# Routed expert tiles: rows gathered by a table of each slot's row number and share, results added by accumulating scatter

## The reference, cut to what matters

```python
x = x + attention0(layernorm(x), ctx)        # 32 heads of 16
x = x + ffn0(layernorm(x))                   # the part that the change touches
x = x + attention1(layernorm(x), ctx)        # 32 heads of 128
x = x + ffn1(layernorm(x))                   # low-rank adapters

def ffn0(x):                                 # x: 1024 tokens x 512
    scores = sigmoid(x @ gate_w.T) + bias    # 16 experts
    topk_w, topk_idx = top_k(scores, 4)
    topk_w = topk_w / sum(topk_w)            # the share of each chosen expert
    cw = one_hot(topk_idx) weighted by topk_w
    z = silu(x @ Wg[e].T) * (x @ Wu[e].T)    # for each expert e, width 256
    out = sum over e of (z * cw[:, e]) @ Wd[e].T
    return out + (silu(x @ Sg.T) * (x @ Su.T)) @ Sd.T     # the shared expert
```

## Time and profile before

| | us |
|---|---|
| median of 3 runs | 1466.79 (1466.39 to 1470.21) |
| profiled execution, its own time | 1462.81 |
| its span, first to last instruction | 1461.2 |
| PE busy | 1275.9 (87%) |
| DVE busy | 965.8 (66%) |
| ACT busy | 812.3 (56%) |
| POOL busy | 389.6 (27%) |
| mean granted TensorE clock | 0.949 of full |
| DMA | 181.72 MB, mean 124 GB/s |

### The profile page before, as it was taken

The page is one execution under the profiler, slowest core; times in us unless marked ns, Lnnn a source line. Parts: engine busy times, 40 slices in busy tenths (PEclk is TensorE's granted clock), DMA queues, the critical chain, the costliest instruction groups (busy, mean ns, idle before and its releaser), DMA issues.

```text
span 1461.2 us, 18404 instructions
## 1 busy us (share of the span) xinstructions
PE 1275.9 (87%) x6250; PEld 1019.9 (70%) x6250; DVE 965.8 (66%) x1889; ACT 812.3 (56%) x2152; POOL 389.6 (27%) x685
## 2 busy tenths in 40 slices
PE   5989998754688888884679999999899999999997
PEld 5667665443566666663568888888778888888875
DVE  5686786522788888884465666667645566667757
ACT  3675786401788888881235555556534555555632
POOL 4454563252000000005302222223201222222300
PEclk7799998976899999998889999999999999999999
DMA  5000180073699999975321111112111111111201
GB/s 205 1 1 1 71 313 1 1 271 122 246 350 345 347 345 344 348 274 165 116 72 47 55 55 56 56 59 65 59 58 58 51 58 59 59 58 58 65 1 58
DMA packets 55806, 181.72 MB, mean 124 GB/s; under 512 B 7008, under 2 KB 7392, under 8 KB 49056
## 3 DMA queue, kind: packets, MB, share of 16 engines
q1 hardware_dynamic: 46832, 151.43, 29.7%
q0 software_dynamic: 8880, 29.11, 5.5%
HBM read 145.38 MB, written 35.13 MB: 124 GB/s over the span
## 4 chain that ended last, share of the span: by engine, by line
PE 70%; DVE 15%; ACT 5%; issue 3%; another core or an unknown queue 2%; POOL 2%; DMA 2%; SPq 0%; ACTq 0%; DVEq 0%; POOLq 0%
PE bank L403 54%; PE bank L1669 6%; DVE wf_lo L997 4%; PE bank L1645 3%; DVE xsT_lo L1121 2%; PE bank L529 2%; PE bank L541 2%; ACT xsT_hi L1116 2%; PE bank L1108 1%; POOL p L873 1%; ACT p L638 1%; DVE x L1340 1%; POOL returned L1329 1%; DVE stats L349 1%
## 5 line engine op out<-in xcount | busy, mean ns | idle before, releaser
L1637 POOL TENSOR_SCALAR p<-p,mx 128x256 f32<-128x256 f32 x256 | 163.3, 654 | 517.3 <-DVE mx L1631 517.3
L403 PE MATMUL bank<-xnA_hi,w1q_hi 128*128 128x512 f32 x288 | 119.2, 414 | 11.3 <-DVE w1q_lo L1458 8.0
L1623 ACT ACTIVATE p<-bank,mx 128x256 f32<-128x256 f32 x256 | 118.2, 486 | 10.9 <-DVE mx L1613 10.7
L997 DVE TENSOR_TENSOR wf_lo<-wf_raw,wf_hi 128x512 fp32r<-128x512 f32 x192 | 123.4, 684 | 0.0
L873 POOL TENSOR_SCALAR p<-p,sx 128x128 f32<-128x128 f32 x256 | 90.3, 372 | 110.6 <-DVE sx L762 110.3
L403 PE MATMUL bank<-wf_hi,xsT_hi 128*128 128x512 f32 x188 | 78.7, 419 | 46.6 <-DVE wf_lo L997 46.6
L403 PE MATMUL bank<-xnA_hi,w1q_lo 128*128 128x512 f32 x288 | 115.0, 399 | 0.0
L403 PE MATMUL bank<-xnA_lo,w1q_hi 128*128 128x512 f32 x288 | 114.4, 397 | 0.0
L1577 ACT ACTIVATE q1T_hi<-bank 128x512 fp32r<-128x512 f32 x64 | 38.2, 597 | 133.6 <-PE bank L403 133.6
L1652 ACT ACTIVATE p1T_hi<-bank 128x512 fp32r<-128x512 f32 x128 | 75.2, 596 | 65.7 <-PE bank L1645 65.7
L992 ACT ACTIVATE wf_hi<-wf_raw 128x512 fp32r<-128x512 f32 x192 | 110.0, 625 | 0.0
(11 more groups left out here) (330 smaller groups left out, 3726.9 us busy)
## 6 DMA issues: line engine op xcount, KB each, us to landing
wf_raw<-in_wffn SPq DMA_DIRECT2D x48, 1536.0 KB
w_raw<-in_wq SPq DMA_DIRECT2D x64, 256.0 KB
w_raw<-in_wo SPq DMA_DIRECT2D x64, 256.0 KB
xs_rows<-xn SPq DMA_DIRECT2D x1, 12032.0 KB, 33.3
xs<-xs_rows SPq DMA_DIRECT2D x47, 256.0 KB, 9.1
ys_rows<-ys POOLq DMA_DIRECT2D x47, 256.0 KB, 5.9
x<-in_x SPq DMA_DIRECT2D x8, 256.0 KB, 7.9
w_raw<-in_wk SPq DMA_DIRECT2D x8, 256.0 KB
```

What stands on the lines that cost most here:

```text
L403: ins = nc.tensor.matmul(ps, a, b, start=(n == 0), stop=(n == len(pairs) - 1))
L997: nc.vector.tensor_tensor(wf[m % 2][1][:, a, c, :], raw[m % 3][:, a, c, :], wf[m % 2][0][:, a, c, :].bitcast(F32), ALU.subtract).then_inc( ...
L1623: ins = nc.scalar.activation(pr1[s % 2][:, h, :], banks.of(("s1", s, n))[:, hh * 2 * P:(hh + 1) * 2 * P], ACT.Exp, bias=m[:, UH + h:UH + h ...
L1637: ins = nc.gpsimd.tensor_scalar(pr1[s % 2][:, h, :], pr1[s % 2][:, h, :], m[:, 3 * UH + h:3 * UH + h + 1], 1.0, ALU.mult, ALU.mult)
```

## The change

Three things, with what hangs on them.

**Gather in place of scatter.** VectorE splits each pair's slot into its tile (`in_tile`, by a multiplication and rounding) and its row in the tile (`at_row`). From these come one-hot tables: `row_hot` (32 pairs x 128 rows; half by VectorE, half by GpSimd) and `tile_hot` (32 pairs x 3 x 48: token number, high and low part of the share). 32 matmuls of 128x144 (`tensor_tokens`) multiply them, and the bank then holds for each slot its token and its share. GpSimd gathers tile j's rows from `xn_rows`, to which SyncE has stored the normalised tokens, four tiles ahead.

**Accumulating scatter.** `scalar_rows_out` multiplies a result with its share. GpSimd adds the 128 rows to `moe` in DRAM by an indirect DMA with `compute_op=ALU.add`; each waits until the one before it has landed. SyncE loads `moe` back in 8 loads, and VectorE adds each with one instruction.

**Order.** The shared expert's steps go in pairs, with the routing arithmetic between them. The eight attention weights are split at the end of the routed tiles, four in each of the last two turns. SyncE's list has all expert weights one after the other, then eleven attention weights, the wait for the last scatter, and the eight returns. Some semaphores are merged to stay within their number; some loads of `x` then wait for four in place of one.

```diff
 def sync_experts():
-    load(xs_rows..., zeros ... TILES).then_inc(S["zero_fill"], 16)
+    load(moe..., zeros ... B + 1).then_inc(S["zero_fill"], 16)
+    for h in range(2):
+        sp.wait_ge(S["xn"], HB * (h + 3))
+        load(xn_rows[h], xn8[:, bs, :]).then_inc(S["st_xn"], 16)
+    sp.wait_ge(S["tile_e"], 1)
+    weights(1)
     sp.wait_ge(S["routed"], 1)
-    for m in (1, 2, 3):
+    for m in range(2, TILES + 1):
         weights(m)
-    for k in range(2 * KT):
+    for k in range(FIRST_LOADS):            # 2 * KT + 3
         sync_weight(k)
-    sp.wait_ge(S["scattered"], 16 * B * TOP0)
-    for j in range(TILES):
-        if j >= 4:
-            sp.wait_ge(S["xs_turned"], j - 3)
-        load(xs[j % 4], xs_rows[j * P:(j + 1) * P, :])
-        if j >= 3:
-            weights(j + 1)
+    sp.wait_ge(S["st_moe"], 16 * TILES)
+    for b in range(B):
+        load(returned[b], moe[b * P:(b + 1) * P, :])
 def scalar_rows_out(n):
-    act.wait_ge(S[f"st_ys{j % Y_RING}"], 16 * (j // Y_RING))
-    nc.scalar.activation(ys[j % Y_RING], bank, ACT.Copy)
+    act.wait_ge(S["st_moe"], 16 * (j - Y_RING + 1))
+    nc.scalar.activation(ys[j % Y_RING], bank, ACT.Copy, scale=share_of[:, j:j + 1])
 def vector_slots():
-    tensor_copy(slots, slot_f)
+    tensor_scalar(shifted, slot_f, 1.0 / P, -(P - 1.0) / (2 * P), ALU.mult, ALU.add)
+    tensor_scalar(shifted, shifted, ROUND, None, ALU.add)
+    tensor_scalar(in_tile, shifted, ROUND, None, ALU.subtract)
+    scalar_tensor_tensor(at_row, in_tile, -float(P), slot_f, ALU.mult, ALU.add)
+def vector_tile_token():                    # two products, 32 x 48 columns each
+def vector_tile_share():                    # two more
+def vector_row_hot():                       # one comparison, 16 x 128 columns
+def gpsimd_row_hot():                       # 16 comparisons of 128 columns
+def tensor_tokens():
+    for i in range(PAIRS):                  # 32
+        nc.tensor.matmul(ps[:, 0:3 * TILE_COLS], row_hot[:, i, :], tile_hot[:, i, :, :], ...)
+def vector_tokens():                        # token_in, token_out, share_of from the bank
+def tensor_shared():
+    tensor_gate_up(0); tensor_gate_up(1)
+    ...                                     # norm turns, gate
+    tensor_z_turn(0); tensor_z_turn(1)
+    tensor_gate_turn(1, ...)
+    tensor_gate_up(2)
+    tensor_ranks()
+    tensor_gate_up(3)
+    for n in (0, 2, 4):
+        if n == 4:
+            tensor_tokens()
+        tensor_down(n); tensor_down(n + 1)
+        tensor_z_turn(n + 2); tensor_z_turn(n + 3)
+        if n < 4:
+            tensor_gate_up(n + 4); tensor_gate_up(n + 5)
+    tensor_down(6); tensor_down(7)
+def vector_shared():
+    ...                                     # norm, choice, z, z_lo of steps 0 and 1
+    vector_slots(); vector_z(2); vector_z(3)
+    vector_tile_e()
+    vector_shared_add(0); vector_shared_add(1); vector_z_lo(2); vector_z_lo(3)
+    vector_shares()
+    vector_tile_token(); vector_z(4); vector_z(5)
+    vector_tile_share(); vector_row_hot()
+    vector_shared_add(2); vector_shared_add(3); vector_z_lo(4); vector_z_lo(5)
+    vector_z(6); vector_z(7)
+    vector_tokens()
+    vector_shared_add(4); vector_shared_add(5); vector_z_lo(6); vector_z_lo(7)
+    for c in range(4):
+        vector_gu(1, c)
+    vector_shared_add(6); vector_shared_add(7)
+    vector_x_lo(0)
 def scalar_experts():                       # and vector_experts
-    if j + 1 == 0:
-        for _ in range(2 * KT):
-            scalar_weight()
+    if j in (TILES - 1, TILES):
+        for _ in range(KT):
+            scalar_weight()
 def gpsimd_experts():
+    def gather(j):
+        if j >= 4:
+            pool.wait_ge(S["xs_turned"], j - 3)
+        indirect_dma_start(out=xs[j % 4], in_=xn_rows, in_offset=token_in[:, j:j + 1])
-    ...                                     # 32 scatters, 47 stores, 32 gathers
+    for j in range(4):
+        gather(j)
+    for j in range(TILES):
+        pool.wait_ge(S["ys"], j + 1)
+        if j:
+            pool.wait_ge(S["st_moe"], 16 * j)
+        indirect_dma_start(out=moe, out_offset=token_out[:, j:j + 1], in_=ys[j % Y_RING],
+                           compute_op=ALU.add).then_inc(S["st_moe"], 16)
+        if j + 4 < TILES:
+            gather(j + 4)
 def vector_return(b):
-    for k in range(TOP0):
-        scalar_tensor_tensor(x[b], returned[b % RETURNS][:, k, :], share[:, b, k:k + 1], x[b], ...)
+    tensor_tensor(x[b], returned[b], x[b], ALU.add)
```

394 lines of the change are left out of this document (248 added, 146 removed).

## The result

The changed kernel takes 1473.03 us in the median of 20 runs (1467.43 to 1479.05), and the kernel before 1466.95 beside it (20 runs, 1458.43 to 1474.04). The ratio is 1.0046, 95% interval 1.0028 to 1.0063: slower by half a per cent, where 1431 us and "faster" had been forecast.

What follows compares the result with a forecast made beforehand. It took routing, VectorE's pace in the tiles (DMA engines 94% busy) and the results' return as open stages before TensorE's 97% busy one. -41 + 37 - 32 = -36 gave 1431 us from the 1466.8 median; range 1390 to 1482.

Steps and rivals of the forecast that it cites:

- Part 1, routing: Ahead of tile 0: scatters and eight attention weights removed, tile 0 at about 335 in place of 376.2, -41 us.
- bound "twice as dear": Routing: if GpSimd's half of `row_hot` cost twice its 11 us, it would end at 323 and cost 5.
- Part 2, tiles: The 47 routed tiles: period rises from 6.09 to 6.9 us by the scatter's landing, +37 us.
- a period is at least the landing of one scatter: Tiles: scatter j waits for scatter j-1 to land, so the landing bounds the period; 6.9 us taken.
- a doubled share of the engines: Tiles: an add has two inputs, so its DMA engine share counts twice, 1.3 us for 0.65.
- that is in time: Tiles: a gather issued 1.3 us after scatter j, its tile turned 7.4 us later, is in time at a 6.3 landing.
- TensorE waiting for `xs`: Tiles: a sign of being wrong, making the gather and not the scatter the late one; no size given.
- Rival (a): Tiles: the scatter isn't the bound, period stays at VectorE's 6.09, time 1394; chance 0.25.
- Rival (b): Tiles, GpSimd's wait on `st_moe`: landing costs more than both ends win, 1482 us at 8.0; chance 0.21.
- the engines' work as a limit: Tiles: DMA engines' work of 6.37 us a tile, at the 0.94 share, makes a period of 6.8.
- Part 3, return: Behind the last tile: gathers and 24 adds removed, queries at G+54 in place of G+85.9, -32 us.
- Rival (c): Tiles: ScalarE's stalls come with every indirect DMA, about ten cost 74 us, ending near no change; chance 0.04.

Runs made afterwards that it cites:

- store_twice_gf: Against the kernel before: tile rows gathered by table, each gather ahead of tile j's wait, plain stores made twice; 1430.53 us beside 1434.05.
- two_sums: Changed kernel with two accumulators in memory, for even and odd tiles, each with its own chain of waits; 1460.58 us, ratio 0.9976.
- four_gathers: Changed kernel with only the first four gathers, later tiles using the rows already in their buffer; 1453.0 us in one run.
- two_sums_gf: Changed kernel with both edits, that of two_sums and that of gather_first; 1418.06 us in one run.
- scatter_no_add: Changed kernel whose scatter writes without accumulating, sums over experts left out, chain of waits kept; 1443.27 us in one run.
- gather_first: Changed kernel with the gather of tile j + 4 issued ahead of the waits for tile j's rows and the scatter before; 1496.17 us, ratio 1.022.

## Why the prediction was wrong

**Part 1, routing: -41 forecast, -36.8 measured.** `at_row`, VectorE's 16.5 us (15.9) and the end of ScalarE's unknown waits came as said. What failed is which list ends last: VectorE's was said to, with the first gather's rows there before it, and it was the gather. Counted from `over`, `token_in` was said for 29.4 us and came at 31.1, the landing of the first gather for 34 to 35 and came at 41.0. Two steps were short. The first is that GpSimd's half of `row_hot` takes 11 us and is hidden. Twelve of its instructions took 0.7 to 1.2 us, four took 1.9 to 4.0, each ending some half us behind the end of one of VectorE's large products; 19.05 in all. The bound "twice as dear" was right about the end (323). The Trainium skill has this case: "SBUF — State Buffer", section "Who interferes with whom", says that a VectorE instruction with two inputs in SBUF contends with a GpSimd instruction that reads SBUF, as its second input comes through the shared read interface. The trace agrees: GpSimd's ninth to twelfth product, beside VectorE's products from 310.36 to 320.31, are the slow ones. The second short step was the first gather, which began 0.9 us behind `token_in` and landed 9.0 us after its issue and not 4.3 + 0.97. The 32 products were priced 7.4 us at the full clock and took 7.08, which is luck: they need 3.77 there and had half of it.

And 23.7 of the 36.8 us (80.1 less 56.4) are ScalarE's unknown waits. Where the chip doesn't have them the new routing is worth 13, an estimate: in store_twice_gf, on such a chip, tile 0 comes 43.5 us behind `over`, as in the changed kernel (43.3).

**Part 2, tiles: +37 forecast, +62.8 measured.** The step that failed is the one from a landing to a period: "a period is at least the landing of one scatter", and then 6.9 was put in for both. What lies between a landing and the beginning of the next scatter was put at nothing, and it is 0.77 us, in 44 of 46 periods. The landing was 6.69 us in the mean and not 6.9. So 46 x 0.77 = 35 us were missing, and 46 x 0.21 = 10 of them came back by the shorter landing: 25 of the 26 by which the part is off. That the landing's size came out is in part luck. It held 0.65 us for a doubled share of the engines; no run shows that share, while the issue of an accumulating scatter, priced 0.97, took 1.61, which is as much more.

The gather's sentence, "that is in time", failed too. The gather's issue begins 1.9 us behind the scatter's, it lands 5.4 us later, 8.0 at most, and TensorE waits 1.2 us for it. TensorE waiting for `xs` had been named as the sign that the gather and not the scatter is the late one. The sign came, and misled: both were late, and the scatter's chain was the longer. The gather sets a period only with the chain away (7.15 in two_sums). Beneath the chain it shows in the landings alone: without gathers they are 0.4 us shorter, 0.47 us of period, 22 us in all (four_gathers, on a chip of the other kind).

Rival (a) had the right period, 6.1, for a kernel with both waits gone, and a wrong reason: landings were 8.9 us there. The Trainium skill's time for one DMA ("DMA: Bandwidth & Descriptors", "Anatomy of one DMA"), 2.6 us for this one, is not met by any landing of a scatter from 400 to 680 us (4.8 at least). What the same page asks of accumulating transfers in "Rules for kernel authors", to wait for the earlier one's semaphore on the same bytes, two accumulators still keep. Rival (b) had the right wait, GpSimd's on `st_moe`, the right side and too long a landing (8.0); with the 0.77 left out it asked for 7.7 before the change loses. At 7.45 a period the change would still have won, had the two ends won 73 us; they won 53.

I counted the engines' work as a limit (6.37 us, a period of 6.8 at the 0.94 share of before); two_sums_gf and store_twice_gf run at 1.00 to 1.02 and VectorE's pace.

**Part 3, return: -32 forecast, -16.2 measured.** Timeline of the changed kernel behind its last gate product, G = 686.10:

```profile
694.86 0.63 ACT L1605 ACTIVATE w1q_hi<-w_raw 128x512 fp32r<-128x512 f32 x1 [3.75 <-DMA w_raw<-in_wk]
...
702.76 0.67 ACT L1131 ACTIVATE ys<-bank,share_of 128x512 f32<-128x512 f32 x1
...
703.73 0.77 PE L428 MATMUL bank<-q1T_hi,w1q_hi 128*128 128x512 f32 x1 [4.19 <-DVE q1T_lo L1613]
...
709.11 3.66 SPq L973 DMA_DIRECT2D returned<-moe  x8
...
719.70 0.47 PE L428 MATMUL bank<-w1o_hi,q1T_hi 128*128 128x512 f32 x1 [2.56 <-DVE w1o_lo L1613]
...
729.58 1.09 PE L408 MATMUL bank<-consts,xn 128*128 128x128 f32 x4 [4.20 <-DVE xn L399]
...
741.77 0.47 PE L428 MATMUL bank<-xnA_hi,w1q_hi 128*128 128x512 f32 x1 [1.66 <-DVE xnA_lo L422]
```

The last eviction begins at G+16.7 (said: result at 12.5), since ScalarE stood for reloads of the ring of three weight buffers three times. The last scatter begins at G+18.2, 0.73 us after the one before has landed, and lands 4.8 us later, so that the loads are issued from G+23.0, said 16.5. The value weights were late by more: values start at G+33.6, said 25. From there the sum allowed 6 us of gaps in 29; measured are 36.1, with TensorE standing 4.20, 1.52, 1.66 and 2.61 us and a clock of 0.95. The terms that were too small are ScalarE's reloads, 2 to 3 us for the first four weights and some more, where the three waits took 3.75, 1.74 and 2.49, and the gaps. Both misses are of size; the order of events was right.

**Parts left out.** 5.7 us are outside all three: the clock before `over`, and the last stage.

**Rival (c)** is out: 94 indirect transfers in the tiles brought no unknown wait. What was said against it, that the waits come with a burst of such transfers, held.

The time lies in the forecast's range (1390 to 1482), but the direction was wrong. All three parts erred to the same side, by 4, 26 and 16 us, and the 0.74 for "faster" was too much.

## What to carry to other kernels

A chain of waits has a period of the landing and of the way from the landing to the next issue: take both from a trace, and count them once for each link. Behind a wait stands everything that its queue issues later. When a wait goes into a queue that also prefetches, put the prefetch ahead of it, and cut the chain at the same time: here each cure alone gave -0.8% or +1.6% of the changed kernel's time, both together -3.7%. When an experiment's number meets a theory, look whether the waits in its trace do as well: a second store gave the period that "load" foretold, by way of a late gather. And when two waits are late at once, follow the chain before you say which sets the pace.

## What the runs showed of the hardware

- The issue of an accumulating indirect scatter took 1.58 to 1.62 us on GpSimd (means of 47), a plain indirect scatter's 1.04 (mean of 47 in scatter_no_add), a gather's 0.94 to 1.5.
- From the landing of a scatter to the beginning of the next one that waited for it went 0.77 us (changed kernel). ScalarE's eviction that waited for the same landing began after 0.08 (gather_first). A scatter that waited for an eviction alone began 0.28 behind its end (two_sums).
- Beside weights at full pace (400 to 600 us) accumulating scatters landed 4.7 to 11.5 us after their issue. They landed latest in the median (8.5 to 8.9) in the three kernels with the shortest periods of all that scatter (6.11 to 6.16).
- GpSimd's product of 128 x 128 takes 0.71 us alone and up to 4.0 beside VectorE's products with two inputs in SBUF.
- TensorE came back at half clock after idling 3.10 to 3.15 us, ahead of 32 products (fourteen traces), and at full clock after 0.88 to 0.91 (four).
- ScalarE's unknown waits (33 us in the kernel before) came with 32 indirect DMAs in a row, on some chips only.
